# Writing out the eight attention chunks of a MoE-attention-MoE block instead of looping over them

## What is computed

```python
x = x + 0.5 * ffn(layernorm(x))      # 64 experts, 6 chosen per token, capacity 256, and a shared one
x = x + attention(layernorm(x))
x = x + 0.5 * ffn(layernorm(x))

# attention: 16 query heads of 32 channels, one key head and one value head shared by all
q = (x @ Wq + bq).reshape(b, s, 16, 32).transpose(0, 2, 1, 3)
k = x @ Wk + bk
v = x @ Wv + bv
scores = einsum('bhsd,btd->bhst', q, k) / sqrt(32)
out = einsum('bhst,btd->bhsd', softmax(scores), v)
return out.transpose(0, 2, 1, 3).reshape(b, s, 512) @ Wo + bo
```

## Time and profile before

| | us |
|---|---|
| median of 3 runs | 3253.41 |
| lowest and highest run | 3252.27 and 3254.57 |
| profiled execution | 3262.69 |
| its span, first to last instruction | 3260.9 |
| attention's main block, about | 815 to 2583 |
| the eight chunks on PE, to the last group | 819.9 to 2513.0 |

### The profile page before, as it was taken

One profiled execution on the slowest core, in us unless ns is written; L12 is line 12 of the kernel. 1 busy time (PEld: TensorE's weight loads), 2 busy tenths in 40 slices (PEclk: granted clock), 3 DMA queues, 4 the chain that ended last, 5 costly groups with the idle time before them and its releaser, 6 DMA issues. The chain is left out here.

```text
span 3260.9 us, 51386 instructions
## 1 busy us (share of the span) xinstructions
PE 2817.5 (86%) x15264; PEld 1629.9 (50%) x15264; DVE 2041.0 (63%) x3922; ACT 1526.6 (47%) x2871; POOL 2219.0 (68%) x1430
## 2 busy tenths in 40 slices
PE   8967777298999998999999989989999875888870
PEld 4644444176555554555555545545555374555540
DVE  7833222267788787787787877877876294333334
ACT  5522222153666565566665655655656452222220
POOL 2158888552788787788787877877878423777770
PEclk9978888699999998999999999999999867999995
DMA  6579999893486676676776766766857254899998
GB/s 217 203 211 247 235 239 236 179 306 134 104 174 138 138 159 130 146 147 135 159 145 131 162 134 146 148 140 136 163 108 160 95 189 171 204 228 236 233 187 318
DMA packets 217038, 576.33 MB, mean 177 GB/s; under 512 B 33981, under 2 KB 35005, under 8 KB 192825
## 3 DMA queue, kind: packets, MB, share of 16 engines
q0 software_dynamic: 87296, 343.98, 52.3%
q1 hardware_dynamic: 125240, 220.55, 20.8%
q10 hardware_dynamic: 4224, 8.39, 0.7%
HBM read 230.94 MB, written 155.24 MB: 118 GB/s over the span
## 5 line engine op out<-in xcount | busy, mean ns | idle before, releaser
L1898 DVE TENSOR_REDUCE attention_mx<-attention_pM 128x1 f32<-128x512 f32 x1984 | 1211.3, 682 | 214.2 <-PE attention_pM L1757 197.5
L1702 ACT ACTIVATE attention_prob<-attention_pS 128x512 f32<-128x512 f32 x2048 | 1035.7, 629 | 570.6 <-PE attention_pS L1744 478.2
L1643 POOL TENSOR_TENSOR attention_pair<-attention_prob 128x1024 f32<-128x1024 f32 x380 | 949.7, 2507 | 196.6 <-ACT attention_prob L1702 185.3
L1744 PE MATMUL attention_pS<-attention_qT,prep_kT 128*128 128x512 f32 x2048 | 841.5, 417 | 26.4 <-issue 20.9
L1757 PE MATMUL attention_pM<-prep_kT,attention_qT 96*128 96x512 f32 x1984 | 809.0, 410 | 3.7 <-issue 3.7
L1744 PEld LDWEIGHTS attention_pS<-attention_qT,prep_kT 128*128 128x128 f32 x2048 | 388.7, 190 | 367.4 <-issue 187.8
L750 POOL DMA_INDIRECT sum<-experts_res,c_table x256 | 404.0, 1578 | 131.5 <-issue 84.7
L1782 PE MATMUL attention_pO<-attention_prob,attention_v 128*32 128x512 f32 x4096 | 492.5, 598 | 0.0
L1757 PEld LDWEIGHTS attention_pM<-prep_kT,attention_qT 96*128 96x128 f32 x1984 | 377.9, 192 | 112.2 <-DVE attention_mx L1898 46.6
L734 POOL DMA_INDIRECT experts_rows<-xn_rows,c_table x256 | 251.5, 982 | 103.9 <-issue 74.1
L779 PE MATMUL experts_pT<-c_ident,experts_rows 128*128 128x128 f32 x1024 | 172.3, 314 | 116.1 <-ACT experts_xT L856 56.5
(11 more groups left out here) (177 smaller groups left out, 2875.1 us busy)
## 6 DMA issues: line engine op xcount, KB each, us to landing
prep_acc<-attention_pair POOLq DMA_DIRECT2D x96, 1024.0 KB, 7.6
attention_acc<-attention_pair POOLq DMA_DIRECT2D x90, 1024.0 KB, 7.6
experts_wup<-in_L_ffn_w_up_dram SPq DMA_DIRECT2D x128, 256.0 KB
attention_qT<-q_parts SPq DMA_DIRECT2D x96, 256.0 KB
xn_rows<-route_xn SPq DMA_DIRECT2D x16, 1152.0 KB, 7.0
experts_wdn<-in_L_ffn_w_down_dram SPq DMA_DIRECT2D x64, 256.0 KB
q_parts<-prep_acc SPq DMA_DIRECT2D x64, 256.0 KB, 4.2
combine_got<-sum SPq DMA_DIRECT2D x16, 1024.0 KB
```

The source lines that it names most:

```text
L1643: pool.tensor_tensor(to[:, part], prob[2 * n % PROBS][:, part], prob[(2 * n + 1) % PROBS][:, part], ALU.add).then_inc(s_pair, 1)
L1702: act.activation(prob[t % PROBS][:, h * QT:(h + 1) * QT], pS[:, at, :], ACT.Exp).then_inc(s_ex, 1)
L1744: pe.matmul(pS[:, at, :], kT[:, key:key + P], qT[g][:, h, :], start=True, stop=True).then_inc(s_sc, 1)
L1898: dve.tensor_reduce(mx[:, unit, part:part + 1], pM[:, r % RING, :], X, ALU.max).then_inc(s_mr, 1)
```

## The change

In `chunks` the two loops and three single bodies give way to a Python loop that emits the body eight times, with integers for `c`. SP's loop over chunks 2 to 7 is written out in the same way. The order of the instructions within each engine, their sizes, the tiles and the semaphores stay as they are.

```diff
--- before.py
+++ after.py
@@ -1535,13 +1535,8 @@
         def chunks(body):
 
             def run(eng):
-                body(0, 0)
-                with eng.Fori(1, CHUNKS // 2 - 1) as c:
-                    body(c, 0)
-                body(CHUNKS // 2 - 1, 0)
-                with eng.Fori(CHUNKS // 2, CHUNKS - 1) as c:
-                    body(c, 1)
-                body(CHUNKS - 1, 1)
+                for c in range(CHUNKS):
+                    body(c, c // (CHUNKS // 2))
             return run
 
         with nc.Block() as block:
@@ -1588,13 +1583,13 @@
                         sp.wait_ge(s_pv, A + (GPC * (c - 1) + (g + 1)) * STEPS)
                         load(sp, c, g)
                         if g == 1:
-                            if not (isinstance(c, int) and c == 1):
+                            if c > 1:
                                 store_x(c - 2)
                             load_x(c - 1)
                         reciprocals(c - 1, g)
 
                 next_chunk(1)
-                with sp.Fori(2, CHUNKS) as c:
+                for c in range(2, CHUNKS):
                     next_chunk(c)
                 for g in range(GPC):
                     if g == 1:
```

## The result

The changed kernel took 3218.23 us, median of 4 runs (3214.49 to 3220.25), beside 3253.99 for the kernel before: a ratio of 0.9888, 95% interval 0.9875 to 0.99, or 35.8 us less (32.5 to 40.7). Measured a second time, in another set of runs, it was 3215.05 beside 3253.96, ratio 0.9878 (0.9861 to 0.9894). The forecast was 3214.8.

A forecast was written before the change was run, and what follows sets the result against it. The prediction took PE to bound the kernel. Jumps back (33.35 us) and computed waits (5.25 us) summed to 38.6 us, taken from 3253.41 us to give 3214.8 us, with a range of 3209 to 3229 us.

The forecast's parts named there:

- Step 1: Attention chunks 2, 5, 6: without PE's three jumps back, their idle time and slow matmuls, 33.35 us are saved.
- Step 2: Five looped attention chunks: without PE's register arithmetic for awaited values, 1.05 us a chunk, 5.25 us in all, are saved.
- Step 3: Loops of DVE, ACT, POOL and SP: removing them costed at nothing further, because these engines wait for PE.
- Step 4: Instruction supply for the longer written-out text: costed at nothing, since executed instructions are fetched either way.

The follow-up runs named there:

- pe_loops: The changed kernel, but PE alone keeps its two loops while DVE, ACT, POOL and SP are written out; ratio 0.9975 to the kernel before.
- pe_one_pass: The changed kernel, but PE's chunks 1, 2, 4, 5, 6 each sit in a loop run once, no branch taken; ratio 0.9886 to the kernel before.

## Why the prediction was right, and where its steps were not

**The sum was right**: 38.6 us by the chunks, 38.7 in the trace, 35.8 and 38.9 in the two sets of medians. It rested on comparing chunks of the same work in the same profile, of which two were already in the form that the change gives to all. Such a difference holds whichever engine causes it.

**Step 1**, the jump, was right: the fetch of far code, not the branch. PE's jumps alone are 29.9 of the 33.35 us. The rest goes when the other engines are written out, nearly all of it in chunk 2 (13.0 us over a looped chunk in before, 9.95 in pe_loops). Part of it is PE's 0.59 us for ACT in the earlier trace rows; which engine brings the remainder no run separates. The Trainium skill, "Advanced Engine Details and Errata", section Control Flow Timing, gives 108 ns for a compare-and-branch, by which the sum would have been an estimated 5.6 us; near jumps took 0.21 to 0.24 us here, twice that figure, and far ones thirty times and more.

**Step 2**, the 5.25 us of computed waits, was right in size and wrong in place: PE's cost nothing (pe_one_pass, pe_loops), DVE's 0.7 us a chunk, ACT's 0.1 to 0.3. I had read the count of register instructions on PE as the cause because PE is the bound. But PE is bound in its array, not in its sequencer.

**Step 3** failed as put: "I cost them at nothing". Alone, ACT's loops cost 24.0 and DVE's 19.5 us. They are small only while PE stalls as well: DVE's lies beside PE's, and ACT's, behind it, took less than half its usual time. The number did not suffer, since the change removed all at once; a forecast for writing out PE alone would have been wrong by 26 us. The sign was in the trace of before: DVE's first reductions of chunk 2 waited 3.8 us for issue, too.

**Step 4** was right where it counts: straight text was fetched in time over all eight chunks. That executed instructions are fetched either way is not quite so: each of PE's jumps back fetched two packets again.

## What to carry over

A loop whose body is longer than what an engine keeps fetched paid at every pass here, on PE, ACT and DVE alike, and the stalls hide one another: writing out, or hinting, only the engine that shows the largest one gives little, because the next takes its place (12 of 38 us here). Look in the profile for "issue" idle right behind a branch, and for neighbouring passes of equal work that differ. To price a change that turns one form of code into another, look first for a stretch that has the other form already.

## What I had not expected

- A branch hint is paid for where the loop is left: 7.6 us at each exit with the hint on PE, 7.2 and 13.4 us with it on four engines.
- The cost of a jump back is a step, not a slope: 0.2 us up to 1700 instructions on PE, 3.8 us at 2600; on ACT 0.2 us at 300 and 2.5 us at 450, where a fetched block is 128 instructions, against PE's 256.
- A far jump took over twice as long on ACT, and nearly twice as long on PE, while the DMA engines were busy: 5.8 to 6.9 us against 2.5 to 2.7, and 6.7 to 7.7 against 3.8. So one engine's stall seems to make a later one cheaper, by leaving the DMA engines idle.
- Register arithmetic of 15.5 us a chunk on PE's sequencer costs nothing at all, while DVE's costs 0.7 us a chunk.
